# A two-layer expert and adapter kernel: the router product moved behind the last LoRA product, and the gates formed ahead of the down masks

## What is computed

```python
def layer0(x, language_ids, W, Wr, A, B):
    base = jnp.einsum('btd,od->bto', x, W)
    logits = jnp.einsum('btd,ed->bte', x, Wr)
    logits = logits + (jax.nn.one_hot(language_ids, 8) * 5.0)[:, None, :]
    topw, topi = jax.lax.top_k(logits, 2)
    weights = jax.nn.softmax(topw, axis=-1)
    gates = jnp.sum(jax.nn.one_hot(topi, 8) * weights[..., None], axis=-2)
    h = jnp.einsum('btd,erd->bter', x, A)                      # rank 16, 8 experts
    return base + 2.0 * jnp.einsum('bter,bte,eor->bto', h, gates, B)

def layer1(x, A, B, adapter_ids):
    Bx = jnp.einsum('bni,bri->bnr', x, B[adapter_ids])         # down, rank 16
    return jnp.einsum('bnr,bor->bno', Bx, A[adapter_ids])      # up

x = x + layer0(x, ...)     # called x1 below
x = x + layer1(x, ...)     # called x2 below
```

## Time and profile before

| | |
|---|---|
| median of 3 runs | 99.46 us (99.19 to 99.73) |
| the profiled execution | 99.71 us |
| its span, first to last instruction | 97.4 us |
| TensorE busy | 92.1 us, 95% |
| VectorE, ScalarE, POOL busy | 62.2, 43.7, 37.4 us |
| HBM read, written | 10.02, 4.19 MB |

### The profile page before, as it was taken

One profiled execution on the slowest core, in us unless ns is written; L12 is line 12 of the kernel. 1 busy time (PEld: TensorE's weight loads), 2 busy tenths in 40 slices (PEclk: granted clock), 3 DMA queues, 4 the chain that ended last, 5 costly groups with the idle time before them and its releaser, 6 DMA issues.

```text
span 97.4 us, 2162 instructions
## 1 busy us (share of the span) xinstructions
PE 92.1 (95%) x733; PEld 77.5 (80%) x733; DVE 62.2 (64%) x215; ACT 43.7 (45%) x88; POOL 37.4 (38%) x44
## 2 busy tenths in 40 slices
PE   4997899999999999999999999999999999999960
PEld 1596788889978788888978898889978897898950
DVE  4163999822297939891089749890199569881980
ACT  2552559240699991089207990099019700000300
POOL 5000778998920049995000069990000370000000
PEclk9999999999999999999999999999999999999999
DMA  1999947438983594235522922227000003241066
GB/s 20 353 279 340 429 156 224 97 73 271 382 202 83 124 367 93 51 71 159 153 60 47 344 98 108 108 50 274 5 0 0 3 7 127 88 172 43 7 211 220
DMA packets 14987, 14.36 MB, mean 147 GB/s; under 512 B 10112, under 2 KB 11392, under 8 KB 14592
## 3 DMA queue, kind: packets, MB, share of 16 engines
q1 hardware_dynamic: 14048, 11.85, 37.9%
q0 software_dynamic: 640, 2.10, 6.9%
q10 hardware_dynamic: 288, 0.28, 1.1%
HBM read 10.02 MB, written 4.19 MB: 146 GB/s over the span
## 4 chain that ended last, share of the span: by engine, by line
PE 84%; DMA 6%; DVE 4%; SPq 1%; ACT 1%; issue 0%; DVEq 0%
PE main L635 16%; PE main L641 15%; PE main L647 15%; PE aw_ps L677 11%; DMA xs<-x_t 6%; PE side L729 6%; PE main L662 4%; PE main L661 4%; PE main L663 4%; PE aw_ps L753 3%; DVE xs L530 2%; PE side L709 2%; PE main L753 1%; PE side L753 1%; SPq L212 1%; DVE x_lo L441 1%
## 5 line engine op out<-in xcount | busy, mean ns | idle before, releaser
L318 POOL TENSOR_TENSOR x_lo<-xs,x_hi 128x512 fp32r<-128x512 f32 x12 | 16.1, 1379 | 19.9 <-ACT x_hi L338 19.9
L635 PE MATMUL main<-x_hi,w_hi 128*128 128x512 f32 (+1 forms) x64 | 17.7, 398 | 0.5 <-DVE w_hi L565 0.5
L641 PE MATMUL main<-x_hi,w_lo 128*128 128x512 f32 (+1 forms) x64 | 16.9, 385 | 0.0
L647 PE MATMUL main<-x_lo,w_hi 128*128 128x512 f32 (+1 forms) x64 | 16.8, 384 | 0.0
L677 PE MATMUL aw_ps<-aws,xs 128*128 128x136 f32 x112 | 14.6, 284 | 0.0
L677 PEld LDWEIGHTS aw_ps<-aws,xs 128*128 128x128 f32 x112 | 14.2, 195 | 0.2
L370 ACT ACTIVATE a_ops<-a_hi 64x512 fp32r<-64x512 f32 x12 | 7.6, 630 | 14.5 <-POOL a_rest L292 14.3
L641 PEld LDWEIGHTS main<-x_hi,w_lo 128*128 128x128 f32 x64 | 11.8, 188 | 2.6
L647 PEld LDWEIGHTS main<-x_lo,w_hi 128*128 128x128 f32 x64 | 11.8, 188 | 2.4
L635 PEld LDWEIGHTS main<-x_hi,w_hi 128*128 128x128 f32 x64 | 11.3, 188 | 2.9 <-DVE w_hi L565 0.7
L489 DVE TENSOR_TENSOR xs<-main,xs 128x512 f32<-128x512 f32 x15 | 9.9, 683 | 2.1 <-PE main L663 2.1
(11 more groups left out here) (107 smaller groups left out, 136.2 us busy)
## 6 DMA issues: line engine op xcount, KB each, us to landing
out_t<-xs SPq DMA_DIRECT2D x16, 256.0 KB, 2.2
xs<-x_t SPq DMA_DIRECT2D x3, 1024.0 KB, 5.3
b1s<-b_t SPq DMA_DIRECT2D x64, 32.0 KB, 2.1
xs<-x_t SPq DMA_DIRECT2D x4, 256.0 KB, 4.1
ws<-w_t SPq DMA_DIRECT2D x4, 256.0 KB, 6.3
b0s<-b_t SPq DMA_DIRECT2D x1, 256.0 KB, 6.5
aws<-aw_t ACTq DMA_DIRECT2D x1, 204.0 KB, 3.9
rows<-a_t,row_at POOLq DMA_INDIRECT x8, 3.6
```

The lines of the kernel that those rows point to most:

```text
L318: nc.gpsimd.tensor_tensor(x_lo[:, t % 2, c], xs[:, t, c], x_hi[:, t % 2, c].bitcast(F32), ALU.subtract).then_inc(x_lo_ready, 1)
L635: nc.tensor.matmul(out_ap, w_hi[:, c, k], x_hi[:, s, k, n], start=(k == 0), stop=False)
L641: nc.tensor.matmul(out_ap, w_lo[:, c, k], x_hi[:, s, k, n], start=False, stop=False)
L647: last = nc.tensor.matmul(out_ap, w_hi[:, c, k], x_lo[:, s, k, n], start=False, stop=False)
```

## The change

On TensorE, `aw_tiles(t + 2)` moves from ahead of `lora(t + 1, 3)` to behind it, directly ahead of the next down products. In the first hand-over it moves from behind `lora(0, 0)` to behind `lora(0, 3)`. On VectorE, `top_two` moves behind all four x1 sums of the tile (from ahead of the last one, or of the last three in the first hand-over), and `gate_h` moves ahead of the two `mask_down`. ScalarE, POOL and SyncE keep their lists.

```diff
@@ -587,15 +587,14 @@
 
                         add_x2(t - 1, range(EARLY, PARTS))
 
-                    if c == (K - 1 if t else 1) and more:
-                        top_two(t + 1)
                     if more or c < K - 1:
                         add_x1(t, c)
                 if more:
+                    top_two(t + 1)
                     pick()
+                    gate_h(t + 1)
                     for g in range(t * GPB, (t + 1) * GPB):
                         mask_down(g)
-                    gate_h(t + 1)
                     for g in range(t * GPB, (t + 1) * GPB):
                         down_rest(g)
                     gt_rest(t + 1)
@@ -781,9 +780,8 @@
             gt_transposes(0)
             base(0, 3)
             for c in range(K):
-                if c == 1:
-                    aw_tiles(1)
                 lora(0, c)
+            aw_tiles(1)
             for t in range(NB - 1):
 
                 for k in range(K - 1):
@@ -804,8 +802,8 @@
                 lora(t + 1, 2)
                 if t + 2 < NB:
                     base(t + 1, 3)
+                    lora(t + 1, 3)
                     aw_tiles(t + 2)
-                    lora(t + 1, 3)
```

## The result

The changed kernel took 100.3 us (median of 5 runs, 100.14 to 100.61) where the kernel before took 99.45 us (5 runs): a ratio of 1.0098, interval 1.0059 to 1.0136. It is slower, by 0.85 us between the medians and 0.97 us by the ratio; 100.15 us was predicted.

The account below looks back on a forecast made before the run. The prediction took TensorE, busy 92.1 of 97.4 us, as the bound, so reordering gains only where it waits. Terms +0.62, +0.03 and +0.03 made +0.68 us on the 99.46 us median: 100.15 us, range 99.6 to 100.7.

Parts of the forecast that it names:

- The first hand-over: Tile 0 to 1: gates still wait for the exponential, masks now follow them, transposes end later: +0.62 us.
- The later hand-overs: Tiles 1 to 2 and 2 to 3: VectorE's masks now set when the transposes end, 54.40 against 54.37: +0.03 us each.
- The x1 wait: Down product of the fourth slice waiting for its x1 sum: goes, 0.09 us in each of two later hand-overs, already swallowed.
- Sum: All hand-overs together: +0.62 + 0.03 + 0.03 = +0.68 us, added to the median.
- TensorE's new wait: Ahead of tile 1's transposes: new idle time of 0.5 to 0.7 us in the changed kernel's profile.
- A sign of being wrong that came true: First hand-over: ScalarE's exponential should still start at about 30.3; the prediction is wrong if it comes earlier.
- POOL rival: First hand-over: an x1 sum blocks POOL's first adapter subtraction, up to 0.44 us more, giving 100.6 us; chance 0.10.
- A new wait behind the masks: Each hand-over's LoRA product waits if down-operand split or rest of gates comes over 0.8 us later than worked out; chance 0.08.
- Faster: Down products' weight loads start at once behind router matmuls: up to 1.1 us back, 98.7 us with half; chance 0.05.
- gains in the later hand-overs: Later transposes don't wait as VectorE's path is 0.15 us or more shorter, each keeping 0.09 us: 99.9 or 99.7; chance 0.12.

Follow-up runs that it names:

- first_only: Kernel before with the whole change in the hand-over from tile 0 to tile 1 alone; ratio 1.0075 to the kernel before.
- after_again: The changed kernel measured once more, on another chip; ratio 1.011 to the kernel before.
- later_only: Kernel before with the whole change in the hand-overs to tiles 2 and 3 alone; ratio 1.002 to the kernel before.
- router_only: Changed kernel with the masks put back ahead of the gates, so only router product and x1 sums moved; ratio 0.9934 to the kernel before.
- before_exp: Kernel before with ScalarE's first-round exponential between the two packings of adapter rows instead of behind both; ratio 0.9931 to the kernel before.
- gates_only: Kernel before with only VectorE's gates moved ahead of the two masks, TensorE's list unchanged; ratio 1.0088 to the kernel before.

## Why the prediction was right, and where its terms were not

- **The first hand-over, +0.62 predicted: +0.74 measured** (3.39 - 2.65). The mechanism is as told: ScalarE's packing, the exponential, gates that stay where they were and masks 0.67 us behind their start (31.49 to 32.16). Two sizes were off. From the last mask to the end of the four transposes it was 33.41 - 32.64 = 0.77 us, not 0.70. Their pace was as estimated: in the time line the four take 0.63 us behind the wait and 0.60 where nothing held them up.

```profile
17.30 0.60 PE L708 MATMUL side<-ident,gated 128*128 128x128 f32 x4
```

What was too small is the time from the release to the first of them, 32.78 - 32.64 = 0.14 us; the 0.48 us of the earlier trace rows, from which the estimate was made, begins at a release behind which the next weight load started after some 0.05 us (32.52 against 32.48). And the denominator started 0.30 us behind the exponential's start, not 0.24. It now waits for two semaphores where it had waited for one, since the masks that stood between took the second. In first_only and after_again it is 0.31 too, in later_only and router_only 0.24; that the second wait is the cause is only argued.
- **The later hand-overs, +0.03 each predicted: +0.13 and +0.11.** The gates started 53.03 - 50.11 = 2.92 us behind the router product, 52.54 - 49.64 = 2.90 predicted; the masks end 0.48 us behind their start as in the earlier trace rows. What was too small is again the step behind the release: 54.95 - 54.18 = 0.77. The other 0.03 us of the first is the gates' 0.02 and as much between the transposes and the end of the router product (50.11 - 33.41 = 16.70 us against 48.95 - 32.96 + 0.69 = 16.68), to the rounding of the rows. The wait of 0.1 to 0.2 us that was to show there came out at 0.27: 0.08 and 0.63 us stand in the chain where 0.44 stood.
- **The x1 wait** is gone: the down products took 1.20 us, not 1.34, which is 0.14 and not 0.09. Their weight loads also no longer start 0.36 us late, and that this has the rest is borne out by the first hand-over, which had no x1 wait: 1.26 us before, 1.16 in router_only. As predicted nothing of it was kept in the changed kernel, because VectorE set the time; with the masks ahead it was kept whole (21.24 and 21.23 us).
- **Sum.** 0.74 + 0.13 + 0.11 = 0.98 us by the terms, 0.97 by the ratio. The sum of 0.68 was right in kind and 0.3 us low. That the largest term applied in full was in part luck: it holds only where the exponential and not TensorE sets T1, the one profile at hand was close to the border (T1 22.96 us behind the first base product, 22.80 in before_exp where nothing waited), and gates_only's profile lies beyond it. The absolute time of T1 in the changed kernel's profile is only 0.45 us later than before (33.41 against 32.96), because the exponential itself came 0.29 us earlier in that execution.
- **TensorE's new wait** ahead of the first transposes was 1.53 us and not 0.5 to 0.7. The prediction took TensorE's time of arrival from one profile. The term did not suffer from it, as the path behind the exponential has no TensorE in it, but the wait did.
- **A sign of being wrong that came true.** The prediction called itself wrong if the exponential came earlier, and it came at 30.02, not 30.31. In the seven profiles with ScalarE's list unchanged it starts between 29.50 and 30.31, with and without the change, so this absolute time could not tell; the time from it to T1 can.
- **POOL rival.** It did not come. POOL's two adapter subtractions took 2.50 us beside the x1 sums, and 2.51 before, where no x1 sum ran beside them; now the sums run from 21.38 to 24.17 and the subtractions from 23.55 on, so for some 0.6 us the two overlapped:

```profile
21.38 2.79 DVE L489 TENSOR_TENSOR xs<-main,xs 128x512 f32<-128x512 f32 x4 [2.12 <-PE main L662]
```

```profile
23.55 2.50 POOL L292 TENSOR_TENSOR a_rest<-rows,a_hi 128x512 f32<-128x512 f32 x2
```

No slowing is seen in this overlap. The Trainium skill ("SBUF — State Buffer", "SBUF: two separate sides") says that a VectorE instruction takes the ports that it shares with GpSimd when it is in a two-port mode or has two SBUF inputs. An x1 sum has one of its two inputs in PSUM, and the 2.50 us agree with that.
- **A new wait behind the masks** did not come. The remainder of the gates was ready at 36.28 and 57.81 us, and the LoRA products that need it stood in the chain at 37.37 and 58.87 without a wait.
- **Faster, and gains in the later hand-overs**: neither, in the changed kernel. The sooner exponential that the first of these asked for was made in before_exp and gave 0.7% on the kernel before. The later hand-overs gain when the masks stay ahead of the gates, as router_only shows.

## What to carry to other kernels

When a piece of work is moved behind another on an engine, ask first what starts the path that it joins. Here the gates of the first hand-over began with an exponential that was queued behind unrelated packing on a third engine, so taking the masks out from ahead of them gained nothing and putting them behind it cost 0.74 us; the same masks behind gates with slack (gates_only in the later hand-overs) cost nothing. And an engine's time of arrival from one profile is one draw: take the events that set a path from the profile, and compare intervals behind them.

## What was not expected of the hardware

A wait of 2.27 us of TensorE was followed by a fall of its granted clock to the 1.2 GHz level, from 34 us or just before until between 37 and 38 us, at a price of some 1.4 us, and two of five runs of that kernel have such a time, with a mean granted clock of 0.983 where the other three have 0.993 to 1.00. A wait of 1.53 us at the same place was followed by no fall in the profile of the changed kernel. And the weight loads of the narrow down products start 0.36 us late behind the 512-column matmuls of the LoRA product, but at once behind the 136-column ones of the router product, 0.05 to 0.10 us per hand-over that no semaphore shows (0.14 less the x1 wait's 0.09, and 1.26 against 1.16 us in the first).
